# Scatter and layer norm of a vision tower with the tokens, not the features, on the partitions

## The chip, the cores and the metric

The kernel runs on one NeuronCore of a Trainium2 chip. A core has five engines with a queue of instructions each: TensorE (PE in the profile; its weight loads are PEld), VectorE (DVE), ScalarE (ACT), GpSimd (POOL) and SyncE (SP), which only starts DMAs. The engines meet at semaphores. SBUF is the working memory of 128 partitions; TensorE writes its results to PSUM, and the others read them there. The metric is the time of one execution on the device in microseconds (us); lower is better.

## What is computed

The reference is a two-layer transformer over 64 images of 65 tokens with 128 features. Each of its four sublayers is added to its input and normalised over the features. This case touches the second one, the first layer's mixture of experts:

```python
def _layernorm(x, axis=-1, eps=1e-05):
    m = jnp.mean(x, axis=axis, keepdims=True)
    v = jnp.var(x, axis=axis, keepdims=True)
    return (x - m) / jnp.sqrt(v + eps)
...
    # _L0_ffn_ref: 16 experts, each takes the k = 8 tokens of an image that suit it best
    gating, index = jax.lax.top_k(affinity, k)
...
    x_e = jnp.einsum('bekh,ehd->bekd', h, w2) + b2[None, :, None, :]
    weighted = gating[..., None] * x_e
    out = jnp.zeros_like(x)
...
    out = out.at[jnp.arange(Bx)[:, None], idx_flat].add(vals_flat)
...
h = _layernorm(h + _L0_ffn_ref(h, ...), axis=-1)
```

For each image there are 16 x 8 = 128 expert rows of 128 features. They are weighted, added up at the token that each belongs to, added to `h`, and normalised token by token.

## The kernel before

The 64 images are worked through in 16 groups of four (`GI = 4`, `GT = 260` tokens). The program is a chain of stages with a barrier between them: embedding and first attention, routing and gathering, the experts, `scatter_and_norm` (lines 896 to 1073), `moving_average`, the second attention, the last stage. `h` is kept twice: `R.h_feat` has the features on the partitions (128 x 260 for a group), `R.h_tok` the tokens (65 x 512). The next stages read both, and `R.base`, which is `h_tok` plus a bias.

In `scatter_and_norm` a group goes through ten steps. The steps are functions inside each engine's program, and every engine calls its own steps in a fixed order for each turn of `pipeline`:

- GpSimd copies the experts' output of the group (`copy`, L926). TensorE turns it (`turn`, L950) and ScalarE saves the turned rows (`to_rows`, L1046).
- VectorE builds the one-hot matrix of the scatter, gate included, one instruction of 128x65 for an image (`placing`, L1003). TensorE multiplies (`scatter`, L960): the rows are the stationary operand and the one-hot moves, so the result has features on partitions and tokens along the row.
- VectorE adds `h_feat` (`residual`, L1011). The mean over features is now a mean over partitions, so TensorE forms it with a matmul by a matrix of 1/128 (`mean`, L968). VectorE subtracts (`centre`, L1019), ScalarE squares (`square`, L1052), TensorE averages again (`var`, L974), ScalarE takes the root (`root`, L1057), and VectorE inverts it and multiplies (`scale`, L1023 and L1028).
- TensorE turns the result to tokens (`tail`, L981). ScalarE saves both forms (`save`, L1061 and L1063), and GpSimd forms `base` (`based`, L932).

The mean and the root come out of the matmul on all 128 partitions, so the inversion works on 128x260 values although only 260 of them differ.

`pipeline(eng, lead, end, start)` writes the first and the last groups out one by one, and puts those between them into a hardware loop of two groups a turn.
## Time and profile before

| | |
|---|---|
| median of 3 runs | 859.21 us (856.6 to 860.98) |
| profiled execution, its own time | 858.74 us |
| its span | 857.0 us |
| TensorE busy | 647.8 us (76%) |
| VectorE busy | 503.9 us (59%) |
| ScalarE busy | 348.4 us (41%) |
| GpSimd busy | 230.8 us (27%) |
| `scatter_and_norm` | from 479.9 to 566.4 us of the span |
| inversions (L1023), 16 of 128x260 | 28.4 us in all |
| mean granted clock of TensorE | 0.818 of full |

Times in the rows count from the span's start. A timeline row has the start, the duration, the engine, the line, the operation, the tiles written and read with their shapes, and the number of instructions merged into the row. In square brackets stands how long the engine was idle just before, and whose instruction ended that. The other 1.7 us of the execution's time lie outside the span. `scatter_and_norm` is about a tenth of the whole, and the change is in it alone.

### The profile page before, as it was taken

What the parts mean: (1) busy time and instruction counts of PE and PEld (TensorE: products, weight loads), DVE (VectorE), ACT (ScalarE), POOL (GpSimd) and SP (SyncE); (2) the same over time, 40 slices, a digit from 0 to 9 for tenths busy, and PEclk for the clock granted to TensorE, in tenths of its full rate; (3) what the DMA queues carried; (4) which work ended last, traced back from release to release, by engine and by line L of the source; (5) the groups of instructions that cost most, each with busy time, mean ns of one, the idle gap of its engine ahead of it and who ended that gap; (6) DMA issues with size and microseconds to landing.
All of it is one profiled execution on the core that took longest, in us unless ns stands there. A gap on an engine that the chain in (4) does not pass through costs nothing. (4 is left out here: it accounts for less than half of the span.)

```text
span 857.0 us, 21432 instructions
## 1 busy us (share of the span) xinstructions
PE 647.8 (76%) x8455; PEld 525.0 (61%) x8455; DVE 503.9 (59%) x904; ACT 348.4 (41%) x871; POOL 230.8 (27%) x270
## 2 busy tenths in 40 slices
PE   2999999999999986730987778668688888982002
PEld 2788888888888865610942466358577777772001
DVE  0375666666666665254212687768677667764862
ACT  0113444444444444210632333432366676666600
POOL 1363333333334440000011233310334443330001
PEclk9999999999999997655579977955698888885555
DMA  8533333333333000027900620000000000001200
GB/s 345 192 147 114 115 114 125 124 128 147 129 132 114 1 2 2 2 98 157 142 8 0 73 29 0 0 1 0 2 2 2 0 0 0 3 2 44 70 12 4
DMA packets 28658, 55.35 MB, mean 65 GB/s; under 512 B 12274, under 2 KB 25698, under 8 KB 26114
## 3 DMA queue, kind: packets, MB, share of 16 engines
q1 hardware_dynamic: 28515, 54.62, 21.4%
q8 instruction: 33, 0.54, 0.3%
q14 instruction: 14, 0.11, 0.0%
q0 software_dynamic: 96, 0.07, 0.0%
HBM read 48.14 MB, written 6.55 MB: 64 GB/s over the span
## 5 line engine op out<-in xcount | busy, mean ns | idle before, releaser
L375 PE MATMUL a_bank<-a_x,a_tok_w 128*128 128x256 f32 (+1 forms) x608 | 150.3, 390 | 15.8 <-DVE a_ht L555 15.8
L375 PEld LDWEIGHTS a_bank<-a_x,a_tok_w 128*128 128x128 f32 (+1 forms) x608 | 113.1, 192 | 37.1 <-DMA tables<-in_tables 15.8
L124 POOL TENSOR_TENSOR a_qt<-a_qp,data 128x512 f32<-128x512 f32 x64 | 71.8, 1153 | 2.1 <-POOL a_qp L617 1.6
L617 POOL TENSOR_TENSOR a_qp<-a_rope 128x260 f32<-128x260 f32 x16 | 11.7, 734 | 175.4 <-DVE a_rope L499 175.4
L1376 ACT ACTIVATE b_at<-b_bank 65x512 f32<-65x512 f32 x64 | 34.8, 601 | 42.8 <-PE b_bank L1223 42.8
L282 ACT ACTIVATE a_at<-a_bank 65x256 f32<-65x256 f32 x128 | 38.8, 389 | 25.9 <-PE a_bank L259 25.9
L493 DVE SCALAR_TENSOR_TENSOR a_ht<-a_bank,data 128x256 f32<-128x256 f32 x16 | 7.7, 483 | 64.3 <-PE a_bank L375 64.3
L1460 POOL TENSOR_TENSOR b_e<-b_e,b_inv 128x585 f32<-128x585 f32 (+1 forms) x32 | 35.5, 1108 | 20.1 <-DVE b_inv L1311 19.8
L259 PE MATMUL a_bank<-a_mix,a_e 64*65 64x64 f32 x1024 | 40.6, 234 | 0.0
L259 PEld LDWEIGHTS a_bank<-a_mix,a_e 64*65 64x65 f32 x1024 | 36.1, 147 | 4.0 <-issue 3.4
L195 ACT ACTIVATE a_e<-a_e 128x390 f32<-128x390 f32 (+1 forms) x48 | 24.3, 510 | 33.2 <-DVE a_e L175 33.2
L1284 DVE TENSOR_TENSOR b_e<-b_scores,tables 128x520 f32<-128x520 f32 x32 | 20.9, 695 | 28.2 <-PE b_scores L1185 28.2
L172 DVE TENSOR_REDUCE a_mx<-a_bank 128x6 f32<-128x390 f32 (+1 forms) x48 | 25.7, 535 | 20.0 <-PE a_bank L146 20.0
L803 PE MATMUL r_bank<-r_pick,r_tok 65*128 65x128 f32 x128 | 27.8, 424 | 12.7 <-DVE r_pick L753 12.7
L1023 DVE RECIPROCAL s_s_rs<-s_s_sd 128x260 f32<-128x260 f32 x16 | 28.4, 1777 | 14.5 <-ACT s_s_sd L1057 14.5
L1110 PE MATMUL c_bank<-h_tok,c_lag 65*65 (+1 forms) x256 | 31.1, 297 | 6.2 <-DVE base L1120 3.2
L1120 DVE SCALAR_TENSOR_TENSOR base<-c_bank,blend,base 65x512 f32 (+1 forms) x16 | 29.6, 1870 | 10.2 <-PE c_bank L1110 10.1
L803 PEld LDWEIGHTS r_bank<-r_pick,r_tok 65*128 65x128 f32 x128 | 27.5, 331 | 12.9 <-issue 12.9
L366 PE MATMUL a_bank<-a_ht,data 128*128 128x260 f32 x128 | 33.9, 388 | 0.8 <-DVE a_ht L493 0.7
L499 DVE SCALAR_TENSOR_TENSOR a_rope<-a_bank,data,tables 128x260 f32<-128x260 f32 x64 | 28.1, 481 | 10.8 <-PE a_bank L366 10.8
L146 PE MATMUL a_bank<-a_kt,a_qt 128*64 128x65 f32 x1024 | 33.4, 223 | 1.3 <-issue 1.2
L1110 PEld LDWEIGHTS c_bank<-h_tok,c_lag 65*65 65x65 f32 x256 | 29.1, 214 | 8.4 <-issue 4.8
(252 smaller groups left out, 1521.5 us busy)
## 6 DMA issues: line engine op xcount, KB each, us to landing
a_x<-in_x SPq DMA_DIRECT2D x16, 2304.0 KB, 7.8
lag_rows<-r_kernel SPq DMA_DIRECT2D x1, 4192.5 KB, 39.2
lags<-lag_rows SPq DMA_DIRECT2D x1, 2112.5 KB
base<-places SPq DMA_DIRECT2D x1, 2080.0 KB
out<-e_plain SPq DMA_DIRECT2D x16, 130.0 KB
expert_weights<-in_w SPq DMA_DIRECT2D x2, 1024.0 KB, 5.8
a_tok_w<-in_tok_w SPq DMA_DIRECT2D x1, 1152.0 KB, 6.7
data<-in_data SPq DMA_DIRECT2D x1, 910.5 KB, 4.8
```

The source lines that it names most:

```text
L124: nc.gpsimd.tensor_tensor(qt[:, b * BLOCKS * P:(b + 1) * BLOCKS * P].rearrange("p (c h i) -> p c h i", i=qb, h=HEADS), wide(by_image[:, b, ...
L146: mm = nc.tensor.matmul(o[r * HALF:(r + 1) * HALF, :], qt[:, at_q:at_q + HALF], kt[:, b * TOKENS:(b + 1) * TOKENS], start=True, stop=True)
L259: mm = nc.tensor.matmul(mixbanks[r][0:TOKENS, col:col + HALF], e[rows, b * BLOCKS + c, :], mix[rows, :], start=True, stop=True)
L282: nc.scalar.activation(own[:, :, r], mixbanks[r][0:TOKENS, cols].rearrange("t (c h i) -> t c h i", c=BLOCKS, h=HEADS), ACT.Copy).then_inc( ...
L366: return nc.tensor.matmul(banks[bank][:, 0:GT], weights, rows, start=True, stop=True)
L375: mm = nc.tensor.matmul(banks[0][:, 0:GP], w[0:rows, k * DIM:(k + 1) * DIM], x[p][0:rows, k * GP:(k + 1) * GP], start=(k == 0), stop=(k == ...
L803: mm = nc.tensor.matmul(banks[p][:, b * P:(b + 1) * P], tok[p][:, b * DIM:(b + 1) * DIM], pick[p][:, b * P:(b + 1) * P], start=True, stop= ...
L1023: nc.vector.reciprocal(rs[p][:, :], sd[p][:, :]).then_inc(S.inverse, 1)
L1110: mm = nc.tensor.matmul(banks[p][0:TOKENS, j * IMAGES:(j + 1) * IMAGES], lag[p][:, j, :], tok[:, :, (2 * i + p) * CH + j], start=True, sto ...
L1120: nc.vector.scalar_tensor_tensor(out=here, in0=banks[p][0:TOKENS, :].rearrange("t (e b) -> t e b", e=CH), scalar=R.blend[0:TOKENS, 1:2], i ...
L1376: nc.scalar.activation(own, turnbanks[q][0:TOKENS, :].rearrange("t (b r i) -> t b r i", b=2, r=STRIPS), ACT.Copy).then_inc(S.at_ready, 1)
L1460: nc.gpsimd.tensor_tensor(e[:, part, :], e[:, part, :], wide(inv[:, part].unsqueeze(2), [P, size, TOKENS]), ALU.mult).then_inc(S.probs_rea ...
```

## The change

The scatter now has the one-hot as the stationary operand and the rows move, so that its result has tokens on the partitions: 65 x 512 for a group. `residual` adds `h_tok` there. Mean and variance become sums along the row: VectorE reduces 65x512 to 65x4 and scales that to minus the mean; ScalarE's new `spread` squares each image's 65x128 with that mean as bias and has the squares summed by the same instruction (`accum_out`), and takes the root of 65x4. VectorE's new `invert` forms the inverse and `shift` = minus mean times inverse, both 65x4. ScalarE's new `normalise` writes the result for each image as `z * rs + shift`. GpSimd reads it from there for `base`, and with one more instruction copies it to `h_tok`. TensorE turns it to features at the end (`tail`), and VectorE saves that (`save_features`). The two matmuls by the matrix of 1/128 are gone.

The order within a turn is new as well. VectorE: invert(g), save_features(g-1), placing(g+2), residual(g+1). ScalarE: normalise(g), to_rows(g+2), spread(g+1). TensorE: scatter(g+1), turn(g+2), tail(g). GpSimd: copy(g+3), based(g-1). The hardware loop now begins at group 2, so groups 2 to 11 are in it.

```diff
-        banks = [ctx.enter_context(nc.psum_tensor(f"s_bank{i}", [P, 512], F32)) for i in range(8)]
-        S = named_semaphores(R.ctx, nc, "s_", "copied turned rows_ready placed z_ready mean_done centred squared "
-                  "var_done sd_ready inverse h_done feat_saved tail_done tok_saved scattered based")
+        banks = [ctx.enter_context(nc.psum_tensor(f"s_bank{i}", [P, 512], F32)) for i in range(6)]
+        S = named_semaphores(R.ctx, nc, "s_", "copied turned rows_ready placed scattered z_ready summed mean_ready "
+                  "squared sd_ready inverse shift_ready h_done tail_done feat_saved based")
...
-        z, zc, sq, sd, rs, hw = ([sb(f"s_{n}{i}", [P, GT]) for i in range(2)] for n in ("z", "zc", "sq", "sd", "rs", "hw"))
+        z = [sb(f"z{i}", [TOKENS, GI, DIM]) for i in range(2)]
+        hw = [sb(f"hw{i}", [TOKENS, GI, DIM]) for i in range(2)]
+        sq = [sb(f"sq{i}", [TOKENS, GI, DIM]) for i in range(2)]
+        total, minus_mean, var, sd, rs, shift = ([sb(f"{n}{i}", [TOKENS, GI]) for i in range(2)]
+                                                 for n in ("total", "mean", "var", "sd", "rs", "shift"))
...
-            def based(n):
-
-                pool.wait_ge(S.tok_saved, n + 1)
-                nc.gpsimd.tensor_tensor(R.base[:, n, :].rearrange("t (b d) -> t b d", b=GI),
-                                        R.h_tok[:, n, :].rearrange("t (b d) -> t b d", b=GI),
-                                        wide(R.bias1[0:TOKENS, :].unsqueeze(1), [TOKENS, GI, DIM]),
-                                        ALU.add).then_inc(S.based, 1)
-
-            for g, i, p in pipeline(pool, 3, GROUPS + 3, 4):
+            def based(n, p):
+
+                pool.wait_ge(S.h_done, n + 1)
+                nc.gpsimd.tensor_tensor(R.base[:, n, :].rearrange("t (b d) -> t b d", b=GI), hw[p][:, :, :],
+                                        wide(R.bias1[0:TOKENS, :].unsqueeze(1), [TOKENS, GI, DIM]), ALU.add)
+                nc.gpsimd.tensor_copy(R.h_tok[:, n, :].rearrange("t (b d) -> t b d", b=GI), hw[p][:, :, :]).then_inc(S.based, 1)
+
+            for g, i, p in pipeline(pool, 3, GROUPS + 1):
                 if exists(g + 3):
                     copy(g + 3, 1 - p)
-                if exists(g - 3):
-                    based(g - 3)
+                if exists(g - 1):
+                    based(g - 1, 1 - p)
...
                 for b in range(GI):
-                    mm = nc.tensor.matmul(banks[2 + p][:, b * TOKENS:(b + 1) * TOKENS],
-                                          rows[p][:, b * DIM:(b + 1) * DIM], put[p][:, b, :], start=True, stop=True)
+                    mm = nc.tensor.matmul(banks[2 + p][0:TOKENS, b * DIM:(b + 1) * DIM], put[p][:, b, :],
+                                          rows[p][:, b * DIM:(b + 1) * DIM], start=True, stop=True)
                 mm.then_inc(S.scattered, 1)
-
-            def mean(n, p):
-                pe.wait_ge(S.z_ready, n + 1)
-
-                wait_past(pe, S.centred, n)
-                nc.tensor.matmul(banks[4][:, 0:GT], T("mean"), z[p][:, :], start=True, stop=True).then_inc(S.mean_done, 1)
-
-            def var(n, p):
-                pe.wait_ge(S.squared, n + 1)
-
-                wait_past(pe, S.sd_ready, n)
-                nc.tensor.matmul(banks[5][:, 0:GT], T("mean"), sq[p][:, :], start=True, stop=True).then_inc(S.var_done, 1)
 
             def tail(n, p):
                 pe.wait_ge(S.h_done, n + 1)
 
-                wait_past(pe, S.tok_saved, n - 1)
+                wait_past(pe, S.feat_saved, n - 1)
                 for b in range(GI):
-                    mm = nc.tensor.transpose(banks[6 + p][0:TOKENS, b * DIM:(b + 1) * DIM],
-                                             hw[p][:, b * TOKENS:(b + 1) * TOKENS], T("ident"))
+                    mm = nc.tensor.transpose(banks[4 + p][:, b * TOKENS:(b + 1) * TOKENS], hw[p][:, b, :],
+                                             T("ident", TOKENS)[:, 0:TOKENS])
                 mm.then_inc(S.tail_done, 1)
 
-            for g, i, p in pipeline(pe, 2, GROUPS + 2, 4):
+            for g, i, p in pipeline(pe, 2, GROUPS + 1):
+                if exists(g + 1):
+                    scatter(g + 1, 1 - p)
                 if exists(g + 2):
                     turn(g + 2, p)
-                if exists(g + 1):
-                    scatter(g + 1, 1 - p)
                 if exists(g):
-                    mean(g, p)
-                if exists(g - 1):
-                    var(g - 1, 1 - p)
-                if exists(g - 2):
-                    tail(g - 2, p)
+                    tail(g, p)
...
             def residual(n, p):
                 dve.wait_ge(S.scattered, n + 1)
 
-                wait_past(dve, S.centred, n - 1)
-                nc.vector.tensor_tensor(z[p][:, :], banks[2 + p][:, 0:GT], R.h_feat[:, n, :], ALU.add).then_inc(S.z_ready, 1)
-
-            def centre(n, p):
+                wait_past(dve, S.h_done, n - 1)
+                nc.vector.tensor_tensor(z[p][:, :, :], banks[2 + p][0:TOKENS, :].rearrange("t (b d) -> t b d", b=GI),
+                                        R.h_tok[:, n, :].rearrange("t (b d) -> t b d", b=GI), ALU.add).then_inc(S.z_ready, 1)
                 dve.wait_ge(S.z_ready, n + 1)
-                dve.wait_ge(S.mean_done, n + 1)
-
-                wait_past(dve, S.squared, n - 1)
+                nc.vector.tensor_reduce(total[p][:, :], z[p][:, :, :], AX.X, ALU.add).then_inc(S.summed, 1)
+                dve.wait_ge(S.summed, n + 1)
+                nc.vector.tensor_scalar(minus_mean[p][:, :], total[p][:, :], -1.0 / DIM, None, ALU.mult).then_inc(S.mean_ready, 1)
+
+            def invert(n, p):
+                dve.wait_ge(S.sd_ready, n + 1)
+
                 wait_past(dve, S.h_done, n - 1)
-                nc.vector.tensor_tensor(zc[p][:, :], z[p][:, :], banks[4][:, 0:GT], ALU.subtract).then_inc(S.centred, 1)
-
-            def scale(n, p):
-                dve.wait_ge(S.sd_ready, n + 1)
                 nc.vector.reciprocal(rs[p][:, :], sd[p][:, :]).then_inc(S.inverse, 1)
                 dve.wait_ge(S.inverse, n + 1)
-
-                wait_past(dve, S.tail_done, n - 1)
-                wait_past(dve, S.feat_saved, n - 1)
-                nc.vector.tensor_tensor(hw[p][:, :], zc[p][:, :], rs[p][:, :], ALU.mult).then_inc(S.h_done, 1)
-
-            for g, i, p in pipeline(dve, 2, GROUPS + 2, 4):
+                nc.vector.tensor_tensor(shift[p][:, :], minus_mean[p][:, :], rs[p][:, :], ALU.mult).then_inc(S.shift_ready, 1)
+
+            def save_features(n, p):
+                dve.wait_ge(S.tail_done, n + 1)
+                nc.vector.tensor_copy(R.h_feat[:, n, :], banks[4 + p][:, 0:GT]).then_inc(S.feat_saved, 1)
+
+            for g, i, p in pipeline(dve, 2, GROUPS + 2):
+                if exists(g):
+                    invert(g, p)
+                if exists(g - 1):
+                    save_features(g - 1, 1 - p)
                 if exists(g + 2):
                     placing(g + 2, p)
                 if exists(g + 1):
                     residual(g + 1, 1 - p)
-                if exists(g):
-                    centre(g, p)
-                if exists(g - 1):
-                    scale(g - 1, 1 - p)
...
-            def square(n, p):
-                act.wait_ge(S.centred, n + 1)
-
-                wait_past(act, S.var_done, n - 1)
-                nc.scalar.activation(sq[p][:, :], zc[p][:, :], ACT.Square).then_inc(S.squared, 1)
-
-            def root(n, p):
-                act.wait_ge(S.var_done, n + 1)
+            def spread(n, p):
+                act.wait_ge(S.mean_ready, n + 1)
+
+                wait_past(act, S.squared, GI * (n - 1))
+                wait_past(act, S.sd_ready, n - 1)
+                for b in range(GI):
+                    nc.scalar.activation(sq[p][:, b, :], z[p][:, b, :], ACT.Square, bias=minus_mean[p][:, b:b + 1],
+                                         accum_out=var[p][:, b:b + 1]).then_inc(S.squared, 1)
+                act.wait_ge(S.squared, GI * (n + 1))
+
                 wait_past(act, S.inverse, n - 1)
-                nc.scalar.activation(sd[p][:, :], banks[5][:, 0:GT], ACT.Sqrt, bias=R.eps[:, :]).then_inc(S.sd_ready, 1)
-
-            def save(n, p):
-                act.wait_ge(S.h_done, n + 1)
-                nc.scalar.activation(R.h_feat[:, n, :], hw[p][:, :], ACT.Copy).then_inc(S.feat_saved, 1)
-                act.wait_ge(S.tail_done, n + 1)
-                nc.scalar.activation(R.h_tok[:, n, :], banks[6 + p][0:TOKENS, :], ACT.Copy).then_inc(S.tok_saved, 1)
-
-            for g, i, p in pipeline(act, 2, GROUPS + 2, 4):
+                nc.scalar.activation(sd[p][:, :], var[p][:, :], ACT.Sqrt, scale=1.0 / DIM,
+                                     bias=R.eps[0:TOKENS, :]).then_inc(S.sd_ready, 1)
+
+            def normalise(n, p):
+                act.wait_ge(S.shift_ready, n + 1)
+
+                wait_past(act, S.tail_done, n - 1)
+                wait_past(act, S.based, n - 1)
+                for b in range(GI):
+                    ins = nc.scalar.activation(hw[p][:, b, :], z[p][:, b, :], ACT.Identity, bias=shift[p][:, b:b + 1],
+                                               scale=rs[p][:, b:b + 1])
+                ins.then_inc(S.h_done, 1)
+
+            for g, i, p in pipeline(act, 2, GROUPS + 1):
+                if exists(g):
+                    normalise(g, p)
                 if exists(g + 2):
                     to_rows(g + 2, p)
-                if exists(g):
-                    square(g, p)
-                if exists(g - 1):
-                    root(g - 1, 1 - p)
-                if exists(g - 2):
-                    save(g - 2, p)
+                if exists(g + 1):
+                    spread(g + 1, 1 - p)
```

VectorE's queue inside the hardware loop, kernel before, second group of the two. `s_s_z` is the sum, `s_s_zc` the centred one, `s_s_sd` the root, `s_s_rs` its inverse, `s_s_hw` the result.

```order
L1003 ISA [waits s_scattered]
L1003 TENSOR_SCALAR s_put<-tables,place_of,gate_of 128x65
...
L1011 ISA [waits s_centred,s_scattered]
L1011 TENSOR_TENSOR s_s_z<-s_bank,h_feat 128x260
L1019 TENSOR_TENSOR s_s_zc<-s_s_z,s_bank 128x260 [waits s_squared,s_h_done,s_mean_done,s_z_ready]
L1023 RECIPROCAL s_s_rs<-s_s_sd 128x260 [waits s_sd_ready]
L1028 TENSOR_TENSOR s_s_hw<-s_s_zc,s_s_rs 128x260 [waits s_feat_saved,s_tail_done,s_inverse]
```

The same place in the changed kernel, first group of the two and the first instruction of the second:

```order
L110 REGISTER_ALU [waits s_sd_ready]
L1009 RECIPROCAL s_rs<-s_sd 65x4 [waits s_h_done]
L1011 TENSOR_TENSOR s_shift<-s_mean,s_rs 65x4 [waits s_inverse]
L1015 ISA [waits s_tail_done]
L1015 COPY h_feat<-s_bank 128x260
...
L998 TENSOR_TENSOR s_z<-s_bank,h_tok 65x512
L1001 TENSOR_REDUCE s_total<-s_z 65x4 [waits s_z_ready]
L1003 TENSOR_SCALAR s_mean<-s_total 65x4 [waits s_summed]
L1009 RECIPROCAL s_rs<-s_sd 65x4 [waits s_h_done,s_sd_ready]
```

The inversion has moved to the head of a turn; it follows the reduction and the mean of the same group directly, and a copy to `h_feat` has come in behind it.

ScalarE's queue in the written-out groups at the end, kernel before:

```order
L1046 ACTIVATE s_yrows<-s_bank 128x512 [waits s_scattered,s_turned]
L1052 ACTIVATE s_s_sq<-s_s_zc 128x260 [waits s_var_done,s_centred]
L1057 ACTIVATE s_s_sd<-s_bank,eps 128x260 [waits s_inverse,s_var_done]
L1061 ACTIVATE h_feat<-s_s_hw 128x260 [waits s_h_done]
L1063 ACTIVATE h_tok<-s_bank 65x512 [waits s_tail_done]
```

and in the changed kernel:

```order
L1055 ACTIVATE s_hw<-s_z,s_shift,s_rs 65x128 [waits s_based,s_tail_done,s_shift_ready]
L1055 ACTIVATE s_hw<-s_z,s_shift,s_rs 65x128 x3
L1033 ACTIVATE s_yrows<-s_bank 128x512 [waits s_scattered,s_turned]
L1041 ACTIVATE s_sq,s_var<-s_z,s_mean 65x128 [waits s_sd_ready,s_squared,s_mean_ready]
L1041 ACTIVATE s_sq,s_var<-s_z,s_mean 65x128 x3
L1046 ACTIVATE s_sd<-s_var,eps 65x4 [waits s_inverse,s_squared]
```

Five instructions for a group have become ten. Before, the root belonged to the group behind the one just squared; now the root follows the four squares of its own group.

## Rows read from the trace of the kernel before

**Rows 1.** Windows: stretch, length, busy PE PEld DVE ACT POOL (instructions), clock, DMA, GB/s.

```profile
500.00:540.50 40.50, 31.82 (x159) 25.39 (x158) 33.32 (x64) 15.11 (x37) 16.11 (x16) 0.78 0.00 0
566.50:603.50 37.00, 31.16 (x257) 29.20 (x257) 29.72 (x17) 10.46 (x16) 0.13 (x1) 0.50 0.00 0
```

**Rows 2.** Waits inside the stage: who waited for whom, us, times, longest.

```profile
DVE s_s_rs L1023 <- ACT s_s_sd L1057: 14.5, 15, 2.3
```

**Rows 3.** Timeline of VectorE, one written-out group behind the loop.

```profile
541.44 1.78 DVE L1023 RECIPROCAL s_s_rs<-s_s_sd 128x260 f32<-128x260 f32 x1 [0.85 <-ACT s_s_sd L1057]
543.25 0.56 DVE L1028 TENSOR_TENSOR s_s_hw<-s_s_zc,s_s_rs 128x260 f32<-128x260 f32 x1
543.74 0.97 DVE L1003 TENSOR_SCALAR s_put<-tables,place_of,gate_of 128x65 f32<-128x65 f32 x4
544.64 0.41 DVE L1011 TENSOR_TENSOR s_s_z<-s_bank,h_feat 128x260 f32<-128x260 f32 x1
544.98 0.41 DVE L1019 TENSOR_TENSOR s_s_zc<-s_s_z,s_bank 128x260 f32<-128x260 f32 x1
546.24 1.78 DVE L1023 RECIPROCAL s_s_rs<-s_s_sd 128x260 f32<-128x260 f32 x1 [0.85 <-ACT s_s_sd L1057]
```

**Rows 4.** Timeline of VectorE inside the loop: an inversion, and another group's placing.

```profile
499.48 1.78 DVE L1023 RECIPROCAL s_s_rs<-s_s_sd 128x260 f32<-128x260 f32 x1 [0.85 <-ACT s_s_sd L1057]
...
512.42 1.26 DVE L1003 TENSOR_SCALAR s_put<-tables,place_of,gate_of 128x65 f32<-128x65 f32 x4
513.60 0.42 DVE L1011 TENSOR_TENSOR s_s_z<-s_bank,h_feat 128x260 f32<-128x260 f32 x1
```

**Rows 5.** Timeline, the stage's ends: first sum, table load, first and last inversion, last `base`.

```profile
483.23 0.43 DVE L1011 TENSOR_TENSOR s_s_z<-s_bank,h_feat 128x260 f32<-128x260 f32 x1
487.94 1.28 ACT L1057 ACT_TABLE_LOAD   x1
489.74 1.78 DVE L1023 RECIPROCAL s_s_rs<-s_s_sd 128x260 f32<-128x260 f32 x1 [2.27 <-ACT s_s_sd L1057]
...
561.01 1.76 DVE L1023 RECIPROCAL s_s_rs<-s_s_sd 128x260 f32<-128x260 f32 x1
565.12 1.26 POOL L932 TENSOR_TENSOR base<-h_tok,bias 65x512 f32<-65x512 f32 x1 [0.75 <-ACT h_tok L1063]
```

**Rows 6.** Groups by form, other stages: busy us, mean ns, idle before.

```profile
L521 DVE TENSOR_TENSOR a_vs<-a_bank,data 65x512 f32<-65x512 f32 x16 | 10.8, 676 | 2.0 <-PE a_bank L396 2.0
L1327 DVE TENSOR_REDUCE b_sums<-b_z 65x4 f32<-65x512 f32 x16 | 10.9, 682 | 0.5
L669 DVE RECIPROCAL r_small<-r_small 128x1 f32<-128x1 f32 x1 | 0.2, 165 | 0.0
L1612 DVE TENSOR_SCALAR e_s<-e_s 64x1 f32<-64x1 f32 x1 | 0.1, 146 | 0.0
L1408 ACT ACTIVATE b_sq<-base 65x128 f32<-65x128 f32 x24 | 7.0, 297 | 0.1
L1663 ACT ACTIVATE e_plain<-base,e_rstd 65x128 f32 x56 | 17.1, 388 | 8.6 <-DMA out<-e_plain 8.6
L1666 ACT ACTIVATE e_s<-e_s,eps 64x1 f32<-64x1 f32 x1 | 0.3, 294 | 38.3 <-DVE e_s L1616 38.3
```

**Rows 7.** Timeline of ScalarE: the second attention's four summed squares (L1408), then `e_plain` (L1663).

```profile
705.59 0.31 ACT L1408 ACTIVATE b_sq<-base 65x128 f32 x1
...
706.69 0.18 ACT L1408 ACTIVATION_READ_ACCUMULATOR b_sq<-base  x1
...
785.94 2.45 ACT L1663 ACTIVATE e_plain<-base,e_rstd 65x128 f32<-65x128 f32 x8 [0.72 <-DVE e_rstd L1554]
```

**Rows 8.** GpSimd's copy of a group by form; a timeline row of four 128-column transposes.

```profile
L926 POOL COPY s_ycp<-yout 128x512 f32 x8 | 6.5, 807 | 0.0
...
557.35 1.12 PE L981 MATMUL s_bank<-tables,s_s_hw 128*65 128x128 f32 x4 [1.11 <-DVE s_s_hw L1028]
```

**Rows 9.** One line's instructions: count, ns min/median/max, first to last start, shapes.

```profile
L1028 DVE TENSOR_TENSOR s_s_hw<-s_s_zc,s_s_rs x16: 430/562/716, 491.6 to 562.8; 128x260 f32<-128x260 f32 x16
```

## The prediction

> **What bounds the kernel now.** The change lives in one stage, so the first question is what sets that stage's pace, not which engine is busiest over the whole span. The busy times by stretch [rows 1] name VectorE: 33.32 of 40.50 us in the stage's loop, while ScalarE has 15.11 and GpSimd 16.11. TensorE shows 31.82, but at a granted clock of 0.78, and its work waits in the rows for others. VectorE still isn't full. The list of waits [rows 2] says where it stands idle: at the inversion, 15 times, 14.5 us in all, for ScalarE's root.
>
> The timeline of one written-out group [rows 3] shows why. Read it as a ring. The inversion starts at 541.44 and the next at 546.24, so a group takes 4.80 us. From start to start, VectorE spends 1.81 on the inversion, 0.49 on the product, 0.90 on the four one-hot instructions, 0.34 on the sum and 0.41 on the centring: 3.95 us. Then it is idle for 0.85 us, in which ScalarE squares and takes a root; VectorE can't go on, because the inversion is next in its queue and wants that root. So the pace is the sum of two legs, **VectorE's work 3.95 plus ScalarE's leg 0.85**. Inside the loop the same ring takes (541.44 - 499.48) / 8 = 5.245 us [rows 3, 4], 0.45 more: the four one-hot instructions take 513.60 - 512.42 = 1.18 there instead of 0.90, and the rest is other register work.
>
> The question for the change is therefore what it does to both legs. A shorter VectorE leg gains nothing if ScalarE's grows by more.
>
> **VectorE's leg after.** In the queue of the changed kernel the ring begins again at the inversion. The steps, with durations from instructions of like shape:
>
> - Inversion of 65x4: 0.165 by the 128x1 one, and 0.03 until the next instruction that needs it, the gap behind the long inversion [rows 3, 6]. 0.20.
> - `shift`, 65x4: 0.15 by the 64x1 one [rows 6]. The copy behind it doesn't wait for it, and such instructions overlap by 0.07 (0.41 long, 0.34 apart, rows 3). 0.08.
> - Copy of 128x260 from PSUM to `h_feat`: 0.34, like the sum of that shape [rows 3]. Its source was turned a group earlier, so no wait.
> - One-hots: 0.90, unchanged.
> - Sum of 65x512 with one operand in PSUM: 0.68 by L521 [rows 6], and 0.03 since the next one waits for it. 0.71.
> - Reduction 65x512 to 65x4: 0.68 by L1327 [rows 6], and 0.03. 0.71. Minus the mean, 65x4: 0.15.
>
> Sum 3.09 us instead of 3.95. Gone are the long inversion (1.81), the product (0.49), the centring (0.41) and the narrower sum.
>
> **ScalarE's leg after.** Here the change pays. Between the mean and the next inversion now stand four squares and a root, in a row and for the same group; nothing else is left for VectorE to do meanwhile. The kernel already has four summed squares of 65x128, in the second attention: from 705.59 to 706.69 + 0.18 = 706.87, so 1.28 us [rows 7]. They have no bias from memory. What does a per-partition scalar from memory cost? No row shows a square with one. For a scale there is the pair 388 against 297 ns at 65x128 [rows 6]: 0.09. So I take 1.28 + 4 x 0.09 = 1.64. The bounds are 1.28 (it hides under the read of the accumulator) and 1.64; I take the upper end, since a bias comes from memory as a scale does, and nothing in the rows says that the read would hide it. The root of 65x4 has a bias too: 0.29, like the 64x1 root of L1666 [rows 6]. With hand-overs of 0.04 on both sides and 0.03 between, **the leg is 0.04 + 1.64 + 0.03 + 0.29 + 0.04 = 2.04 us** instead of 0.85.
>
> The Trainium skill, "ScalarE: Activation LUTs", section "What ACT_TABLE_LOAD costs", states 186 ns plus 0.833 ns for each element, about 93 ns more for each such pointer operand. The rows' 297 and 388 ns at 128 elements agree with it (293 and 386). By it the bias would cost the same in a square, and the sum would be the one just made; without it, at the lower bound, the leg would be 1.68.
>
> **The pace.** Written out: 3.09 + 2.04 = **5.13 us** against 4.80. In the loop the one-hots add 0.28; before, other register work added 0.17, and now there is more of it (two more addresses on VectorE, a register instruction at ScalarE's wait for the mean in each group and at the root's in every other). I take 0.23 for it, with bounds 0.1 and 0.4: **5.64 us** against 5.245. And ten groups instead of eight are in the loop.
>
> **The whole stage.** From first to last inversion before: 561.01 - 489.74 = 71.27 us [rows 5]. After: the first interval has no copy to features (5.13 - 0.34 = 4.79), one of 5.13, ten of 5.64, two of 5.13, and the last has no one-hots (4.23). Sum 80.81: **9.54 us more**.
>
> Fill: the first sum starts at 483.23 [rows 5]; the wider scatter makes it 483.4. The mean is there at 483.4 + 1.57 = 484.97, the squares end at 486.65, the table load of 1.28 follows as it does now, and the first inversion starts at 488.3 instead of 489.74: **1.45 less**. Drain: before, from the last inversion to the end of the last `base`, 565.12 + 1.26 - 561.01 = 5.37. After: 0.35 for inverse and shift, 0.04, 1.64 for `normalise` (four of 65x128 with two scalars from memory; with one they stand (2.45 - 0.39) / 7 = 0.295 apart [rows 7], so 0.385 with two, and the last is 0.48 long), 0.04, 1.21 for `base` and 0.75 for GpSimd's new copy (0.807 at 128x512, rows 8): 4.03, **1.34 less**.
>
> Net 9.54 - 1.45 - 1.34 = +6.75 us. On the profiled execution's 858.74 us that is **865.5 us**; that execution stands 0.5 below the median of 859.21, too little to correct for.
>
> **What I cost at nothing, and its cover.** ScalarE's `normalise` and `to_rows`, 1.64 + 0.5 from 0.4 us behind the inversion, end at about 2.6; the mean comes at 3.09 or later, so 0.5 us of cover is left, and whatever exceeds it would lengthen the ring one for one. GpSimd has 0.81 + 1.26 + 0.75 = 2.8 us for a group of over 5. TensorE loses two matmuls and its scatter doubles its columns. Four 128-column transposes took 1.12 us at 557.35 [rows 8], shortly ahead of the stage with a granted clock of 0.50 [rows 1], so I take it for the price at the low clock; eight such instructions of scatter make 2.2, `turn` 1.1 and `tail` 1.1 at most. The result is ready 2.05 behind the inversion, turned at 3.2, and the next scatter done at 5.4; VectorE wants it at 5.6 + 1.8 = 7.4. That is 2 us of cover, even at the low clock. `moving_average` and everything behind it have the same instructions as before; the former already ran at a clock of 0.50 [rows 1], so less work on TensorE ahead of it has nothing to take away there.
>
> **Rivals.**
>
> *The leg of ScalarE is shorter than I sum it* (no change). If the bias costs nothing beside the accumulator, the squares take 1.28 and `normalise` 1.28. The ring is 0.36 shorter, 15 x 0.36 + 0.36 in the fill + 0.36 in the drain = 6.1 us: 859.4 us. For it speaks that in such a series the read of the accumulator may cover something; against it the 0.09 of the scale [rows 6]. Chance 0.20.
>
> *The pace is set by throughput, not by the ring* (faster). It decides whether VectorE has to stand idle while ScalarE squares. If the squares of one group could run under the one-hots of the next, the busiest engine would set the pace: ScalarE with 1.54 + 0.5 + 1.56 + 0.3 = 3.9 us, some 4.2 with its waits. Sixteen groups at 1.0 us less than now give 843 us. Against it speaks the queue: the inversion stands directly behind the mean of its own group. It would take an order that isn't there. Chance 0.05.
>
> *GpSimd disturbs VectorE* (slower still). Its work grows by 0.75 us and now falls on the sum and the reduction. The product of two SBUF tiles varies from 0.43 to 0.72 us in this stage [rows 9], beside GpSimd's copies in some groups; if the sum suffers the same, about 0.26 a group, 16 groups add 4.2 us: 869.7. Against it: the sum reads one operand from PSUM, and such sums are 0.41 throughout. Chance 0.12.
>
> *The 128x260 steps were never the cost, and the change moves nothing.* That would need ScalarE's leg hidden and VectorE's unchanged; the ring excludes it but for chance, 0.03.
>
> By the Trainium skill, "VectorE: DVE Perf Modes", section "The TRN2 errata — SBUF-src ops pay a fixed extra latency per instruction", many small tiles pay a latency that a single large one pays once. It speaks against eight 65x128 instructions where two of 128x260 stood; the rows' 297 ns for 128 elements show this fixed part, and the sum has it in.
>
> **How the numbers follow.** Forecast 865.5 with a chance of 0.60; its own spread, from the register work (0.1 to 0.4 for each of ten groups) and small terms, is about 862.5 to 868.5. The range reaches to the rival of no change and nearly to the slowest: 859.2 to 870.0. A measurement of this kernel can tell about 0.5%, 4.3 us, from no change. Above 863.5 lie most of the forecast and the GpSimd rival: slower 0.65. Between 854.9 and 863.5 lie the short leg, the rest and the low edge of the forecast: same 0.28. Faster 0.07.
>
> **What would show it right or wrong.** In the profile after: inversions (L1009) 5.1 us apart in the written-out groups and 5.6 in the loop; idle time of about 2 us before each, ended by ScalarE's root (L1046); in the waits, some 32 us in that one row instead of 14.5; VectorE's busy time in the stage down by a fifth; squares 0.39 apart. The forecast is wrong if the squares are 0.30 apart, if the first wait in the list is for TensorE or GpSimd, if ScalarE comes late to the squares because `normalise` isn't done, or if the second attention's length differs.

## The result: slower by more than forecast

The changed kernel takes 870.13 us (median of 4, 868.59 to 871.8) against 859.6 for the kernel before. The ratio is 1.0128, with a 95% interval from 1.0094 to 1.0161. The direction was forecast and is clear of noise; 865.5 was forecast, with 870.0 as the upper end of the range. The growth is 10.5 us and not 6.75.

The profiled execution spans 868.8 us, 11.8 more. Where it lies is soon found: `scatter_and_norm` now runs from 480.8 to 579.8 us. That is 99.0 us where it was 86.5 [rows 5], 12.5 more; everything ahead of it is 0.9 later, and everything behind it takes 1.6 less, as two executions of the same program also differ. Cut at the first and the last inversion, the stage shows which part of the sum failed:

| | before | forecast | measured after |
|---|---|---|---|
| stage start to first inversion | 9.8 | 8.4 | 8.2 |
| first to last inversion (15 intervals) | 71.27 | 80.81 | 86.82 |
| last inversion to end of stage | 5.37 | 4.03 | 3.96 |

Fill and drain are as summed, to 0.2 us. All that is missing, 6.0 us, is in the pace. Here is one written-out group of the changed kernel on VectorE, the answer to [rows 3], with GpSimd's rows among them (timeline: start, duration, engine, line, operation, tiles and shapes, idle before):

```profile
560.54 0.17 DVE L1009 RECIPROCAL s_rs<-s_sd 65x4 f32<-65x4 f32 x1 [2.18 <-ACT s_sd L1046]
560.75 0.16 DVE L1011 TENSOR_TENSOR s_shift<-s_mean,s_rs 65x4 f32<-65x4 f32 x1
560.83 0.42 DVE L1015 COPY h_feat<-s_bank 128x260 f32<-128x260 f32 x1
561.17 0.97 DVE L990 TENSOR_SCALAR s_put<-tables,place_of,gate_of 128x65 f32<-128x65 f32 x4
562.06 0.68 DVE L998 TENSOR_TENSOR s_z<-s_bank,h_tok 65x512 f32<-65x512 f32 x1
562.67 1.29 POOL L936 TENSOR_TENSOR base<-s_hw,bias 65x512 f32<-65x512 f32 x1 [3.78 <-ACT s_hw L1055]
562.78 0.68 DVE L1001 TENSOR_REDUCE s_total<-s_z 65x4 f32<-65x512 f32 x1
563.50 0.49 DVE L1003 TENSOR_SCALAR s_mean<-s_total 65x4 f32<-65x4 f32 x1
563.91 0.60 POOL L938 COPY h_tok<-s_hw 65x512 f32<-65x512 f32 x1
564.02 0.40 ACT L1041 ACTIVATE s_sq<-s_z,s_mean 65x128 f32<-65x128 f32 x1 [0.95 <-DVE s_mean L1003]
...
565.20 0.39 ACT L1041 ACTIVATE s_sq<-s_z,s_mean 65x128 f32<-65x128 f32 x1
565.49 0.19 ACT L1041 ACTIVATION_READ_ACCUMULATOR s_sq<-s_z,s_mean 65x1 f32 x1
565.71 0.30 ACT L1046 ACTIVATE s_sd<-s_var,eps 65x4 f32<-65x4 f32 x1
566.04 0.17 DVE L1009 RECIPROCAL s_rs<-s_sd 65x4 f32<-65x4 f32 x1 [2.05 <-ACT s_sd L1046]
```

The ring is there as described, with VectorE idle for 2.18 and 2.05 us before the two inversions, ended by ScalarE's root. The period is 566.04 - 560.54 = 5.50 us instead of 5.13. From the end of the mean at 563.99 to the next inversion it is 2.05 us; 2.04 was summed, and the squares are 0.39 apart. So ScalarE's leg is right to a hundredth, and the difference lies on VectorE, in one row: minus the mean, 65x4, takes 0.49 us instead of 0.15. It starts at 563.50 and ends at 563.99. GpSimd's sum for `base` runs from 562.67 to 563.96. The small instruction ends just when GpSimd's does.

In the loop it is worse:

```profile
500.46 0.61 POOL L930 COPY s_ycp<-yout 128x512 f32 x1 [1.54 <-PE s_bank L953]
500.52 0.17 DVE L1009 RECIPROCAL s_rs<-s_sd 65x4 f32<-65x4 f32 x1 [2.13 <-ACT s_sd L1046]
500.73 0.35 DVE L1011 TENSOR_TENSOR s_shift<-s_mean,s_rs 65x4 f32<-65x4 f32 x1
501.00 0.41 DVE L1015 COPY h_feat<-s_bank 128x260 f32 x1
501.34 0.97 DVE L990 TENSOR_SCALAR s_put<-tables,place_of,gate_of 128x65 f32<-128x65 f32 x4
502.23 0.68 DVE L998 TENSOR_TENSOR s_z<-s_bank,h_tok 65x512 f32<-65x512 f32 x1
502.94 0.68 DVE L1001 TENSOR_REDUCE s_total<-s_z 65x4 f32<-65x512 f32 x1
503.08 1.29 POOL L936 TENSOR_TENSOR base<-s_hw,bias 65x512 f32 x1 [2.01 <-ACT s_hw L1055]
503.66 0.73 DVE L1003 TENSOR_SCALAR s_mean<-s_total 65x4 f32<-65x4 f32 x1
506.58 0.17 DVE L1009 RECIPROCAL s_rs<-s_sd 65x4 f32<-65x4 f32 x1 [2.19 <-ACT s_sd L1046]
```

Here the shift too is long, 0.35 us, and ends at 501.08, when GpSimd's copy ends at 501.07; the mean ends at 504.39, GpSimd's sum at 504.37. The period is 6.06. And a third thing is to be seen: the four one-hots take 0.97, not the 1.26 of [rows 4], though they have the same register instructions between them. Those of [rows 4] ran from 512.42 beside a copy of GpSimd, and these run beside none:

```profile
512.15 0.81 POOL L926 COPY s_ycp<-yout 128x512 f32 x1
```

Meanwhile the reduction (L1001) takes its 0.68 beside GpSimd's sum, and the inversion its 0.17 beside GpSimd's copy. Not every instruction is held up. Of the sum (L998) the changed kernel says little, since in the steady groups it lies beside GpSimd for 0.12 us at most.

### The profile page after: what moved, and what is told of

Same layout as the page of the kernel before. It is cut to its first block and busy times, and to the rows that moved or that the text cites. A ratio compares the mean times of both kernels' runs of the same rounds, so it can differ in the third digit from the quotient of the medians.

```text
span 868.8 us, 21509 instructions
## 1 busy us (share of the span) xinstructions
PE 634.7 (73%) x8391; PEld 517.8 (60%) x8391; DVE 494.9 (57%) x936; ACT 379.9 (44%) x1015; POOL 238.9 (27%) x286
## 5 line engine op out<-in xcount | busy, mean ns | idle before, releaser
L972 PE MATMUL s_bank<-tables,s_hw 65*128 65x65 f32 x64 | 10.2, 306 | 45.6 <-ACT s_hw L1055 45.6
L972 PEld LDWEIGHTS s_bank<-tables,s_hw 65*128 65x128 f32 x64 | 7.4, 197 | 51.6 <-ACT s_hw L1055 35.9
```

## The experiments

Theory A: the stage is a ring of two legs, and VectorE's small instructions wait for the end of whatever GpSimd is doing. Rivals are that the mean is slow because it reads what the reduction has just written, and that all of it is register work of the loop. Each run is compared with runs of the kernel before on the same chip, whose median was 862.86 us beside e1 to e4 and 859.8 beside e5 to e8; so the ratios are to be read, not the medians. The ratios are those on record with their intervals; the quotients of the medians given here differ from them by up to 0.0017 (1.0122 for the changed kernel, 1.0044 for e1, 0.9894 for e4). The column for the loop is the mean of the ten intervals from the second inversion to the twelfth, for e5 of the eight from the third to the eleventh. The kernel before has 5.25 us in those eight and 4.80 behind the loop.

| run | median us | ratio to before (95%) | inversion to inversion in the loop | behind it, written out |
|---|---|---|---|---|
| changed kernel | 870.13 | 1.0128 (1.0094 to 1.0161) | 6.04 | 5.50 |
| e1, no `based` on GpSimd | 866.66 | 1.0032 (1.0013 to 1.0052) | 5.54 | 5.16 |
| e2, row sums in PSUM | 866.2 | 1.0031 (1.0009 to 1.0052) | 5.45 | 5.16 |
| e3, sum first | 873.01 | 1.0108 (1.0073 to 1.0142) | 4.9 to 6.1 | 7.0, 5.5 and 4.4 |
| e4, one square | 853.72 | 0.9877 (0.983 to 0.9923) | 4.70 | 4.46 |
| e5, kernel before, centre first | 849.7 | 0.9877 (0.9847 to 0.9906) | 4.26 | 3.94 |
| e6, all orders changed | 878.57 | 1.0222 (1.02 to 1.0243) | 6.48 | 6.16 |
| e7, changed kernel written out | 866.62 | 1.0083 (1.0058 to 1.0108) | 5.64 (5.5 and 5.7) | 5.5 |
| e8, sum first, one-hots a group earlier | 852.03 | 0.9909 (0.9878 to 0.9941) | 4.56 | 4.43 |

**e1: take GpSimd's work away.**

```diff
-                if exists(g - 1):
-                    based(g - 1, 1 - p)
...
-                wait_past(act, S.based, n - 1)
```

> The changed kernel, but GpSimd leaves out its step `based`: base and h_tok are not written in this stage, so those values are missing from what follows. Only copy is left to GpSimd. Theory A (VectorE's instruction for minus the mean, L1003, waits for the end of GpSimd's sum for base): L1003 falls from 0.45-0.83 us to 0.17, the ring from 5.49 to 5.15 us in the written-out groups and from 6.04 to about 5.55 in the loop; with the shorter drain some 7 us off, about 863 us. Theory B (L1003 is slow because it reads what the reduction has just written, or through the loop's register work): L1003 stays at 0.45 and more, only the drain is shorter, about 869.5 us.

The ratio falls from 1.0128 to 1.0032, about 8 us; from first to last inversion it is 80.14 us instead of 86.82, and the drain is shorter by 0.7. The mean takes 0.17 us in every group, and a written-out group 5.16: the forecast's 5.13, without the disturbance. Theory B, that the mean is slow because of what it reads or through register work, fell: both are as before.

**e2: leave GpSimd as it is, and take VectorE out of its way.** The reduction writes its four sums to PSUM, and mean and shift read them there. No instruction is saved, and the same values are computed.

```diff
...
-                nc.vector.tensor_reduce(total[p][:, :], z[p][:, :, :], AX.X, ALU.add).then_inc(S.summed, 1)
+                nc.vector.tensor_reduce(banks[6 + p][0:TOKENS, 0:GI], z[p][:, :, :], AX.X, ALU.add).then_inc(S.summed, 1)
                 dve.wait_ge(S.summed, n + 1)
-                nc.vector.tensor_scalar(minus_mean[p][:, :], total[p][:, :], -1.0 / DIM, None, ALU.mult).then_inc(S.mean_ready, 1)
+                nc.vector.tensor_scalar(minus_mean[p][:, :], banks[6 + p][0:TOKENS, 0:GI], -1.0 / DIM, None, ALU.mult).then_inc(S.mean_ready, 1)
...
-                nc.vector.tensor_tensor(shift[p][:, :], minus_mean[p][:, :], rs[p][:, :], ALU.mult).then_inc(S.shift_ready, 1)
+                nc.vector.scalar_tensor_tensor(out=shift[p][:, :], in0=banks[6 + p][0:TOKENS, 0:GI], scalar=-1.0 / DIM,
+                                               in1=rs[p][:, :], op0=ALU.mult, op1=ALU.mult).then_inc(S.shift_ready, 1)
```

> The changed kernel with the row sums in PSUM instead of SBUF: the reduction writes there, minus the mean and the shift read there. The same numbers are computed; GpSimd works as in the changed kernel. Theory A1 (VectorE waits for GpSimd only with instructions that want SBUF through both read ways: one source at double speed, or two SBUF sources): minus the mean takes about 0.2 us, the shift 0.16, ring 5.15 written out and about 5.5 in the loop, about 862 us. Theory A2 (any small instruction of VectorE waits while GpSimd works): no change, 870 us. Theory B (the wait is for the reduction's result): no change, 870 us.

The timeline of a written-out group:

```profile
560.87 1.27 POOL L936 TENSOR_TENSOR base<-s_hw,bias 65x512 f32<-65x512 f32 x1 [3.33 <-ACT s_hw L1056]
560.97 0.69 DVE L1001 TENSOR_REDUCE s_bank<-s_z 65x4 f32<-65x512 f32 x1
561.69 0.16 DVE L1003 TENSOR_SCALAR s_mean<-s_bank 65x4 f32<-65x4 f32 x1
561.89 0.40 ACT L1042 ACTIVATE s_sq<-s_z,s_mean 65x128 f32<-65x128 f32 x1 [0.61 <-DVE s_mean L1003]
562.08 0.61 POOL L938 COPY h_tok<-s_hw 65x512 f32<-65x512 f32 x1
```

The mean now runs in the middle of GpSimd's 1.27 us and takes 0.16. It is the same small instruction at the same place, and only the memory of its source has changed. Ratio 1.0031, the gain of e1, while GpSimd does all its work. Theory A2, that any small instruction waits, fell too: what matters is where the operands are. For the shift this is shown less cleanly: its instruction was changed with its operand, and it met GpSimd's copy in only five groups; it took 0.16 there too. Over all 16 groups, the line of the mean in the changed kernel and then in e2 (count, ns shortest/median/longest):

```profile
L1003 DVE TENSOR_SCALAR s_mean<-s_total x16: 165/606/833, 485.5 to 573.6; 65x4 f32<-65x4 f32 x16
```

```profile
L1003 DVE TENSOR_SCALAR s_mean<-s_bank x16: 157/157/158, 485.4 to 566.0; 65x4 f32<-65x4 f32 x16
```

From first to last inversion e2 takes 568.16 - 488.88 = 79.28 us where the changed kernel takes 86.82. The mean and the shift give back 8.5 us of their waits; 0.75 is lost again, because in a few groups of the loop it is now the one-hots that meet GpSimd's copy (1.27 us at 494.33 instead of 0.97). That covers the 6 us.

**e7: the loop.** All 16 groups are written out:

```diff
-            for g, i, p in pipeline(dve, 2, GROUPS + 2):
+            for g, i, p in written_out(2, GROUPS + 2):
```

(and so on the three other engines; `written_out` is a plain Python loop over the groups).

> The changed kernel with all 16 groups of this stage written out, without the hardware loop; the same instructions otherwise. Theory L (the 0.55 us by which a group of the loop, 6.04, is longer than a written-out one, 5.49, is register work): all groups take 5.5 us, 10 x 0.55 = 5.5 us off the changed kernel, ratio to the kernel before about 1.006. Theory G (part of it is GpSimd's copy of the next group meeting VectorE's shift, and more of its sum meeting the mean, whatever the loop): groups in the middle stay at 5.7 to 5.9, 2 to 3 us off, ratio about 1.010.

It came out between the two theories, at 1.0083. There are two kinds of groups, from 5.47 to 5.50 us and, mostly two in a row, from 5.68 to 5.75; one stands between them at 5.59. The long ones are those where the shift meets GpSimd's copy of the next group:

```profile
517.66 0.61 POOL L936 COPY s_ycp<-yout 128x512 f32<-128x512 f32 x1 [1.50 <-PE s_bank L959]
517.69 0.17 DVE L1015 RECIPROCAL s_rs<-s_sd 65x4 f32<-65x4 f32 x1 [2.05 <-ACT s_sd L1052]
517.90 0.39 DVE L1017 TENSOR_TENSOR s_shift<-s_mean,s_rs 65x4 f32<-65x4 f32 x1
518.21 0.41 DVE L1021 COPY h_feat<-s_bank 128x260 f32<-128x260 f32 x1
```

So of the 0.55 us by which a group of the loop is longer, about 0.15 are such meetings and 0.4 come with the loop; that part holds longer waits at the mean as well, mostly 0.60 to 0.74 against 0.50. How much of the 0.4 is register work alone isn't shown; in e2, where neither mean nor shift waits, a loop group that meets nothing takes 5.35 or 5.45 against 5.16, so 0.2 to 0.3.

**e4: does ScalarE's leg count one for one?** One square of 65x512 stands in for the four summed ones.

```diff
-                for b in range(GI):
-                    nc.scalar.activation(sq[p][:, b, :], z[p][:, b, :], ACT.Square, bias=minus_mean[p][:, b:b + 1],
-                                         accum_out=var[p][:, b:b + 1]).then_inc(S.squared, 1)
...
+                nc.scalar.activation(sq[p][:, :, :], z[p][:, :, :], ACT.Square).then_inc(S.squared, 1)
...
-                nc.scalar.activation(sd[p][:, :], var[p][:, :], ACT.Sqrt, scale=1.0 / DIM,
+                nc.scalar.activation(sd[p][:, :], sq[p][:, :, 0], ACT.Sqrt, scale=1.0 / DIM,
```

> The changed kernel with ScalarE's four summed squares of 65x128 replaced by one square of 65x512 without bias and without a sum; the root reads four of its values, so the variance is not computed and what follows has other values. Theory A (ring): ScalarE's leg falls from 2.05 to about 1.0 us, each group is 1.05 shorter, 15 x 1.05 + 1.05 in the fill = 17 us off, about 853 us. Rival (ScalarE's squares are hidden behind another engine): less than 5 us off, above 865 us.

The variance isn't computed then, so this is a probe and not a version to keep. It does: a written-out group falls from 5.50 to 4.46 us, by 1.04. VectorE's idle time before the inversion is 1.03 instead of 2.05. The whole gains more than expected, ratio 0.9877 against 1.0128; in the loop the groups fell by 1.34. Of the 18.7 us that are gone between the first and the last inversion, 16.6 are ScalarE's leg, and 2.1 come from mean, shift and one-hots, which now meet GpSimd at other points. This leg alone, in its form of four short instructions, costs more than the whole change lost.

**e3, e8 and e6: put work between the mean and the inversion.** If the ring is the cause, VectorE's copy and one-hots should run while ScalarE squares. e3 changes the order on VectorE alone:

```diff
                 if exists(g):
                     invert(g, p)
+                if exists(g + 1):
+                    residual(g + 1, 1 - p)
                 if exists(g - 1):
                     save_features(g - 1, 1 - p)
                 if exists(g + 2):
                     placing(g + 2, p)
-                if exists(g + 1):
-                    residual(g + 1, 1 - p)
```

> The changed kernel with another order on VectorE alone: residual(g+1), with sum, reduction and mean, directly behind invert(g), and the copy to features and the one-hots behind it. Theory A (the stage is a ring of VectorE's leg and ScalarE's leg): the 1.25 us of copy and one-hots run while ScalarE squares; then ScalarE's own queue closes the ring (normalise 1.65, to_rows 0.49, squares 1.6, root 0.3, hand-overs 0.4): 4.45 us written out, about 4.75 in the loop, some 18 us off, about 852 us. Rival T (TensorE's scatter now comes late: tail 0.7 and scatter 1.94 behind normalise): ring about 5.0, 858 us. Rival R (the pace is set by something else than this ring): unchanged, 870 us.

It gained nothing clear of noise (1.0108 against 1.0128). That is rival R's number, but not its reason: e4 had shown this ring to set the pace of the changed kernel, and the trace of e3 shows that another one took its place:

```profile
505.17 1.27 POOL L936 TENSOR_TENSOR base<-s_hw,bias 65x512 f32 x1
505.27 0.43 DVE L1015 COPY h_feat<-s_bank 128x260 f32 x1
505.49 0.40 ACT L1041 ACTIVATE s_sq<-s_z,s_mean 65x128 f32<-65x128 f32 x1 [0.45 <-DVE s_mean L1003]
505.62 1.87 DVE L990 TENSOR_SCALAR s_put<-tables,place_of,gate_of 128x65 f32<-128x65 f32 x4
...
507.50 0.17 DVE L1009 RECIPROCAL s_rs<-s_sd 65x4 f32<-65x4 f32 x1
507.54 1.97 PE L963 MATMUL s_bank<-s_yrows,s_put 128*65 128x128 f32 x8 [2.70 <-DVE s_put L990]
...
509.67 0.69 DVE L998 TENSOR_TENSOR s_z<-s_bank,h_tok 65x512 f32<-65x512 f32 x1 [1.80 <-ACT s_hw L1055]
```

The inversion has no idle time left here, as wanted, and in ten of the 16 groups. But the one-hots now are the last thing ahead of the scatter that needs them, and TensorE takes 1.97 us for it after they are ready; VectorE waits for that before the sum, which starts at 509.67, 0.16 after the scatter's end at 509.51. The row names ScalarE's `normalise` in its place, which ended at 509.55; but this sum doesn't need it, as e8 shows, where it starts before `normalise` has ended. And one-hots that run beside GpSimd's sum take 1.87 us, not 0.97. In e8 the one-hots are therefore built for the group behind (with the sums in PSUM, as in e2):

```diff
...
-            for g, i, p in pipeline(dve, 2, GROUPS + 2):
+            for g, i, p in pipeline(dve, 3, GROUPS + 2):
                 if exists(g):
                     invert(g, p)
+                if exists(g + 1):
+                    residual(g + 1, 1 - p)
                 if exists(g - 1):
                     save_features(g - 1, 1 - p)
-                if exists(g + 2):
-                    placing(g + 2, p)
-                if exists(g + 1):
-                    residual(g + 1, 1 - p)
+                if exists(g + 3):
+                    placing(g + 3, 1 - p)
```

> The changed kernel with the row sums in PSUM, residual(g+1) directly behind invert(g), and the one-hots built a group earlier, placing(g+3), so that TensorE's scatter finds them ready. Theory A (ring): copy and one-hots now run while ScalarE squares; ScalarE's own queue (normalise 1.65, to_rows 0.49, squares 1.6, root 0.3, hand-overs 0.4) sets 4.45 to 4.8 us for a group, ratio to the kernel before about 0.99. Rival (the one-hots now wait for GpSimd's sum and copy, 1.87 us instead of 0.97, and VectorE or TensorE closes another ring of 5.5 us and more): ratio 1.003 or above.

Groups of 4.43 and 4.56 us, ratio 0.9909 (0.9878 to 0.9941), faster than the kernel before by just under 1%. What the earlier one-hots and the sums in PSUM each give isn't separated. It is ScalarE's queue now that closes the ring, as expected: `normalise`, `to_rows`, squares and root, with no idle time between them but the 0.43 to 0.66 us from root to `normalise`, in which VectorE inverts and forms the shift. e6 tried to shorten that ring by squaring ahead of `to_rows`, and by moving TensorE's `tail` and the copy to features a group back (only ScalarE's part is shown):

```diff
...
+                if exists(g + 1):
+                    spread(g + 1, 1 - p)
                 if exists(g + 2):
                     to_rows(g + 2, p)
-                if exists(g + 1):
-                    spread(g + 1, 1 - p)
```

> As the kernel with sums in PSUM and one-hots a group earlier, and also: ScalarE squares before it saves the turned rows, TensorE turns the result back a group later, behind the next scatter, and VectorE copies it to features a group later. Theory A (two legs, each now with the other engine's work beside it): the ring is normalise, squares, root and hand-overs on ScalarE, 4.0 to 4.3 us a group, ratio to the kernel before about 0.983. Rival T (TensorE at its lower clock, scatter 1.95, turn 1.06, tail 0.7, sets 4.6 and more): ratio about 0.99.

It is the slowest of all, 1.0222, and the expectation had overlooked a dependency. The scatter needs the rows, and they are now saved last:

```profile
520.62 0.30 ACT L1047 ACTIVATE s_sd<-s_var,eps 65x4 f32<-65x4 f32 x1
520.82 0.57 ACT L1034 ACTIVATE s_yrows<-s_bank 128x512 f32<-128x512 f32 x1
...
521.64 1.87 PE L963 MATMUL s_bank<-s_yrows,s_put 128*65 128x128 f32 x8 [3.35 <-ACT s_yrows L1034]
...
523.66 0.69 DVE L998 TENSOR_TENSOR s_z<-s_bank,h_tok 65x512 f32<-65x512 f32 x1 [2.35 <-PE s_bank L963]
```

Rows, scatter, sum, reduction, mean, squares, root, and then the next rows: the whole group in one ring of 6.5 us.

Late in the stage of e6 VectorE's sum, which has one operand in PSUM, starts and ends while GpSimd's runs, and isn't held:

```profile
568.62 1.28 POOL L936 TENSOR_TENSOR base<-s_hw,bias 65x512 f32<-65x512 f32 x1 [2.75 <-ACT s_hw L1056]
569.00 0.69 DVE L998 TENSOR_TENSOR s_z<-s_bank,h_tok 65x512 f32<-65x512 f32 x1 [2.14 <-PE s_bank L963]
```

**e5: the same trick on the kernel before.** Its ring has 0.85 us of idle time [rows 3]; the centring moves ahead of the one-hots and the sum:

```diff
+                if exists(g):
+                    centre(g, p)
                 if exists(g + 2):
                     placing(g + 2, p)
                 if exists(g + 1):
                     residual(g + 1, 1 - p)
-                if exists(g):
-                    centre(g, p)
                 if exists(g - 1):
                     scale(g - 1, 1 - p)
```

> The kernel before with another order on VectorE alone: centre(g) ahead of placing(g+2) and residual(g+1), so that 1.24 us of work lie between the centring and the inversion, in which ScalarE squares and takes the root. Theory A (the kernel before is such a ring as well): its 0.85 us of idle time before each inversion go, ring 3.95 instead of 4.80 written out, 16 x 0.85 = 13 us off, ratio 0.985. Rival T (TensorE, 6.3 us of work for a group at the lower clock, then has the mean late): 4 to 6 us off, ratio 0.994. Rival R (the idle time is filled otherwise): no change.

```profile
542.83 0.42 DVE L1019 TENSOR_TENSOR s_s_zc<-s_s_z,s_bank 128x260 f32<-128x260 f32 x1
543.17 0.98 DVE L1003 TENSOR_SCALAR s_put<-tables,place_of,gate_of 128x65 f32<-128x65 f32 x4
544.06 0.42 DVE L1011 TENSOR_TENSOR s_s_z<-s_bank,h_feat 128x260 f32<-128x260 f32 x1
544.40 1.77 DVE L1023 RECIPROCAL s_s_rs<-s_s_sd 128x260 f32<-128x260 f32 x1
```

No idle time is left ahead of the inversion, here and in 13 of the 16 groups; a group takes 3.94 us written out, as summed (3.95). Ratio 0.9877 (0.9847 to 0.9906), with the same instructions in another order. It beats both kernels and has the lowest ratio of the versions that compute the result, though its interval overlaps that of e8: two lines moved on the kernel before do about as much as all of e8 on the changed one.

## Why the prediction was wrong in size

The 15 intervals from first to last inversion, added up step by step (from start to start; the mean by its duration, and what follows it up to the inversion as ScalarE's leg with the register work):

| step | forecast | changed kernel | e2 |
|---|---|---|---|
| inversion | 3.00 | 3.13 | 3.12 |
| shift | 1.20 | 3.44 | 1.64 |
| copy to features | 4.76 | 4.75 | 4.81 |
| one-hots | 15.40 | 12.48 | 13.23 |
| sum | 10.65 | 10.68 | 10.69 |
| reduction | 10.65 | 10.79 | 10.89 |
| minus the mean | 2.25 | 9.08 | 2.40 |
| ScalarE's leg, register work | 32.90 | 32.47 | 32.50 |
| all | 80.81 | 86.82 | 79.28 |

- **The bound.** Right. The stage is a ring of VectorE's and ScalarE's legs. Shown by e4 (a cut of ScalarE's leg comes back one for one), and by e5 and e8 (work moved under that leg comes back).
- **ScalarE's leg, 2.04 us.** Right: 2.05 written out, and 2.13 to 2.27 in the loop, where part of the register work falls on it. Each square with its bias from memory is 0.39 apart, so the upper bound was the value. The rival of the short leg is out.
- **VectorE's leg, 3.09 us.** The step that failed is its small terms: "Minus the mean, 65x4: 0.15" and the 0.08 for `shift`. I priced them from a row of a stage in which GpSimd wasn't busy. The wait for GpSimd stood in the sum at nothing. The runs showed in its place a median of 0.61 us for the mean and 0.34 for the shift, because they waited for GpSimd: 6.83 us more than summed for the mean and 2.24 for the shift.
- **The loop's extra.** "In the loop the one-hots add 0.28" was read rightly from [rows 4], but its cause was wrong. At 512.42 those one-hots met GpSimd's copy of 512.15 to 512.96. In the changed kernel they don't meet it, and take 0.97 in the loop. That is 2.9 us less than the forecast. The two errors have the same cause and partly cancel: 6.83 + 2.24 - 2.92 = 6.15. With the other steps, -0.14 together, that is the 6.01 us missing.
- **The rival "GpSimd disturbs VectorE".** It was the case that came, but at other instructions. I had it hit the sum, which reads one operand from PSUM, and had named that as the reason against it. The sum is indeed untouched (e6); the tiny instruction behind it isn't. That its time, 869.7, lies near the measured one is luck: it was 4.2 us on the sum, and what came was 9.1 on mean and shift and -2.9 on the one-hots.
- **Covers.** TensorE's granted clock was 0.56 on average between 500 and 555 us, near the lower of its two levels (1.2 GHz, 0.5 of full), against 0.78 in the loop before [rows 1], and its work stayed hidden; ScalarE was idle for 0.95 to 1.2 us ahead of the squares in nearly all groups, so `normalise` and `to_rows` didn't lengthen the ring. Both held, as fill and drain did. Two of the signs were off: the wait for the root came to 35.8 us and not 32, and VectorE's busy time in the stage fell from 67.4 to 58.3 us, by 14% and not by a fifth, since the time in which an instruction is held counts as busy.

The trace of the kernel before would have given the answer. [rows 9] shows a product of two SBUF tiles at 0.43 to 0.72 us. I put that down to GpSimd's copies and carried it over to the sum, instead of asking which instructions vary, and beside what. In 14 of its 16 groups the product starts while GpSimd's sum for `base` runs and ends 0.28 to 0.30 us after that sum's end; in the two others, which start while no such sum runs, it takes 0.43.

## What to carry to other kernels

An instruction's work is not its price on a ring: write down the order of each queue, find the leg in which the other engine has nothing to do, and put independent work there before rewriting the arithmetic. Check each move for what it feeds (one-hots ahead of the scatter, rows ahead of the scatter), since in e3 and e6 the idle time only moved. When VectorE and GpSimd both work on SBUF, compare the ends of their instructions, not their busy shares; a 65x4 instruction on the path can cost as much as a 65x512 one.

## What the runs showed of the hardware

- In these runs VectorE's instructions waited for the end of a running GpSimd instruction if they had two operands in SBUF (shift, 0.16 alone, up to 0.51) or were a fp32 tensor-scalar from SBUF (mean, 0.17 alone, up to 0.83; four one-hots, 0.97 alone, 1.87 in e3). Sums with one operand in PSUM and reductions weren't held beside GpSimd's sum, nor the inversion of 65x4 beside its copy (0.69 in e6, 0.68, 0.17). With its source in PSUM the mean took 0.16 beside GpSimd. The Trainium skill, "SBUF — State Buffer", section "SBUF: two separate sides", says that VectorE and GpSimd share one pair of ports under an exclusive lock that is held for a whole instruction, against VectorE's two-port modes and instructions with two SBUF inputs; the traces agree: the mean of 563.50 ends at 563.99, 0.03 after GpSimd's sum. Read against GpSimd's queue, it names the instructions to suspect; what they cost hangs on where they meet.
- A summed square of 65x128 with a bias from memory costs 0.39 us in a row of four. The summed squares without such a bias in [rows 7] are 0.30 apart, so 0.09 goes with the bias.
